# A Swin window block on one core: scores of four images at once, gelu as one image and then three, and the values of a chunk made in the first half of its own period

## What is computed

```
xw = windows of x                                  # 64 tokens of 32 channels each
q, k, v = split(ln1(xw) @ qkv_w.T + qkv_b)         # 4 heads of 8
attn = softmax(q * hd**-0.5 @ k.T + bias)          # 64x64 for each window and head
xw = xw + (attn @ v) @ proj_w.T + proj_b
h = gelu(ln2(xw) @ fc1_w.T + fc1_b)                # 128 hidden
xw = xw + h @ fc2_w.T + fc2_b
```

## Time and profile before

| | us |
|---|---|
| median of 3 runs | 189.28 |
| lowest, highest | 188.22, 192.5 |
| the profiled execution's own time | 188.29 |
| its span, first to last instruction | 186.6 |
| busy: PE, ACT, DVE, POOL | 169.2, 129.2, 120.2, 91.4 |
| TensorE's granted clock, mean | 0.998 of full speed |

### The profile page before, as it was taken

One profiled execution on the slowest core, in us unless ns is written; L12 is line 12 of the kernel. 1 busy time (PEld: TensorE's weight loads), 2 busy tenths in 40 slices (PEclk: granted clock), 3 DMA queues, 4 the chain that ended last, 5 costly groups with the idle time before them and its releaser, 6 DMA issues.

```text
span 186.6 us, 6349 instructions
## 1 busy us (share of the span) xinstructions
PE 169.2 (91%) x2688; PEld 92.4 (50%) x2688; DVE 120.2 (64%) x220; ACT 129.2 (69%) x180; POOL 91.4 (49%) x103
## 2 busy tenths in 40 slices
PE   7976999999999999999999999999999878738882
PEld 7642465566456546565565565455655533102210
DVE  3486965978687677869786977677697821403222
ACT  4546595569677866868696779677843385798881
POOL 7402674647492856567484937584766540020000
PEclk9999999999999999999999999999999999999999
DMA  2840000000000000000000000000000000001323
GB/s 71 231 174 4 0 2 4 4 4 2 4 4 0 4 4 2 4 5 0 4 4 4 0 4 5 0 4 0 4 5 4 0 4 0 29 27 56 116 112 112
DMA packets 3245, 4.71 MB, mean 25 GB/s; under 512 B 946, under 2 KB 1298, under 8 KB 3218
## 3 DMA queue, kind: packets, MB, share of 16 engines
q1 hardware_dynamic: 2840, 4.23, 6.7%
q0 software_dynamic: 256, 0.07, 0.4%
q10 hardware_dynamic: 122, 0.01, 0.0%
HBM read 2.21 MB, written 2.10 MB: 23 GB/s over the span
## 4 chain that ended last, share of the span: by engine, by line
PE 67%; DVE 10%; ACT 10%; issue 5%; DMA 3%; POOL 3%; ACTq 1%; DVEq 0%; POOLq 0%
PE ps L670 17%; PE ps L686 12%; PE ps L605 9%; PE ps L704 9%; PE ps L711 7%; DVE s_sb L477 7%; ACT hid L342 5%; PE ps L651 4%; PE ps L751 4%; PE ps L629 3%; DMA raw_b<-in_L_conv_rpb_dram 3%; POOL raw_b L193 2%; DVE mx L487 1%; ACT rstd L330 1%; ACT pt L255 1%
## 5 line engine op out<-in xcount | busy, mean ns | idle before, releaser
L211 POOL TENSOR_TENSOR s_sb<-s_sb,mx 128x512 f32<-128x512 f32 x64 | 66.6, 1045 | 61.1 <-DVE mx L487 61.1
L477 DVE TENSOR_TENSOR s_sb<-ps,bias_t 128x512 f32<-128x512 f32 x64 | 43.9, 686 | 26.0 <-PE ps L670 25.0
L487 DVE TENSOR_REDUCE mx<-s_sb 128x8 f32<-128x512 f32 x64 | 43.9, 686 | 2.2
L670 PE MATMUL ps<-k_m,q_sb 32*64 32x256 f32 x512 | 35.0, 387 | 2.9 <-DVE s_sb L477 2.1
L686 PEld LDWEIGHTS ps<-ident,s_sb 128*128 128x128 f32 x256 | 27.5, 140 | 17.7 <-issue 10.3
L255 ACT ACTIVATE pt<-ps 128x1024 f32<-128x1024 f32 x32 | 32.5, 1016 | 5.1 <-PE ps L686 4.2
L686 PE MATMUL ps<-ident,s_sb 128*128 128x128 f32 x256 | 34.9, 279 | 0.0
L670 PEld LDWEIGHTS ps<-k_m,q_sb 32*64 32x64 f32 x512 | 16.4, 131 | 15.2 <-DVE s_sb L477 5.6
L704 PEld LDWEIGHTS ps<-pt,v_blk 128*32 128x32 f32 x1024 | 15.0, 110 | 8.1 <-ACT pt L255 6.0
L704 PE MATMUL ps<-pt,v_blk 128*32 128x64 f32 x1024 | 17.6, 220 | 1.5 <-ACT pt L255 1.5
L342 ACT ACTIVATE hid<-ps,fb 128x1024 f32<-128x1024 f32 x16 | 17.0, 1110 | 2.0 <-PE ps L751 2.0
(11 more groups left out here) (92 smaller groups left out, 190.5 us busy)
## 6 DMA issues: line engine op xcount, KB each, us to landing
x_sb<-in_x_dram SPq DMA_DIRECT2D x8, 256.0 KB, 4.8
out_dram<-y_sb SPq DMA_DIRECT2D x7, 256.0 KB, 2.0
out_dram<-y_sb SPq DMA_DIRECT2D x2, 128.0 KB, 1.8
raw_b<-in_L_conv_rpb_dram POOLq DMA_DIRECT2D x8, 8.0 KB, 2.7
f_nat<-in_L_conv_fc_w_dram SPq DMA_DIRECT2D x2, 16.0 KB
w_nat<-in_L_conv_qkv_w_dram ACTq DMA_DIRECT2D x1, 12.0 KB
p_nat<-in_L_conv_proj_w_dram SPq DMA_DIRECT2D x1, 4.0 KB
vec_r<-in_L_conv_ln_g_dram ACTq DMA_DIRECT2D x1, 0.1 KB
```

What stands on the lines that cost most here:

```text
L211: pool.tensor_tensor(tile, tile, mx[:, n % 4, :].unsqueeze(2).to_broadcast([128, 2 * NH, NT]), ALU.subtract).then_inc(shifted, 1)
L477: dve.tensor_tensor(s_sb[:, n % NSB, :, :, :].rearrange("p a h m -> p a (h m)"), S_PS[u].rearrange("p (a k) -> p a k", a=2), bias_t[:, :, ...
L487: dve.reduce_max(mx[:, n % 4, :], s_sb[:, n % NSB, :, :, :].rearrange("p a h m -> p (a h) m"), AX.X)\
L670: ins = pe.matmul(S_PS[u][NT * ab:NT * (ab + 1), 256 * pr:256 * (pr + 1)], q_sb[C * g:C * (g + 1), c % 2, NT * w:NT * (w + 1)], k_m[C * g: ...
```

## The change

Eight units a chunk stay, but their scores are made in two calls of four images (`score(c, t)`, t the half of the windows), into four banks. That takes two banks more, so the others are shared anew: `S_PS` is banks 0 to 3, `T_PS` 4 and 5, and only `X_PS` (bank 6) and `Y_PS` (bank 7) are left. The first variance goes to score bank 0 between the scores' two calls, q to bank 0 behind the second, v to bank 1 between the calls, the first half of attention to bank 1 behind the second; the second normalization, the projection and the second half of attention are all in `Y_PS`. New waits guard the shared banks: among them `score(c, 0)` waits for `divided` of the chunk before, `score(c, 1)` for `v_copied` of its own chunk. v of chunk c is made in period c and not in period c-1. `inv_std2` is cut in two, with `exp_round` between its logarithm (`log_var2`) and its exponential. `gelu` reads one bank (the shared one) and then three. `up(0)` goes ahead of the last `attend`. Nothing else of the arithmetic changes.

The core of the diff:

```diff
-        S_PS = [ps[:, 0, :], ps[:, 1, :]]
-        T_PS = [ps[:, 2, :], ps[:, 3, :]]
-        FA, FB = ps[:, 4, :], ps[:, 5, :]
-        O_PS, D_PS = ps[:, 6, :], ps[:, 7, :]
-        OD_PS = [O_PS, D_PS]
...
+        S_PS = [ps[:, g, :] for g in range(G)]
+        T_PS = [ps[:, 4, :], ps[:, 5, :]]
+        X_PS, Y_PS = ps[:, 6, :], ps[:, 7, :]
+        OD_PS = [S_PS[1], Y_PS]
...
+        def unit_of(c, t, g):
+            return 8 * c + 4 * t + g
...
-            def inv_std2(p):
+            def log_var2(p):
                 act.wait_ge(var2_ready, p + 1)
                 if p >= 1:
                     act.wait_ge(h2_ready, p)
-                act.activation(rstd2[:, :], FB, ACT.Ln, bias=eps[:, :]).then_inc(log2, 1)
+                act.activation(rstd2[:, :], Y_PS, ACT.Ln, bias=eps[:, :]).then_inc(log2, 1)
+
+            def inv_std2(p):
                 act.wait_ge(log2, p + 1)
...
-                for pair in ((1, 0) if low(c) else (0, 1)):
-                    b = first_bank(c) + 2 * pair
-                    act.activation(hid[:, c % 2, 2 * pair:2 * pair + 2, :].rearrange("p g n -> p (g n)"),
-                                   ps[:, b:b + 2, :].rearrange("p g n -> p (g n)"),
+                shared = 3 - first_bank(c)
+                for images in (slice(shared, shared + 1), slice(0, 3) if low(c) else slice(1, 4)):
+                    banks = slice(first_bank(c) + images.start, first_bank(c) + images.stop)
+                    act.activation(hid[:, c % 2, images, :].rearrange("p g n -> p (g n)"),
+                                   ps[:, banks, :].rearrange("p g n -> p (g n)"),
                                    ACT.Gelu, bias=fb1[:, :]).then_inc(gelu_ready, 1)
...
-                if there(p):
-                    inv_den(p, 0)
                 if there(f):
                     square1(f)
                 if c == 0:
                     blank_values(1)
                 if there(p - 1):
+                    log_var2(p - 1)
+                if there(p):
+                    exp_round(p, 3)
+                if there(f):
+                    inv_std1(f)
+                if c >= 1 and there(c):
+                    copy_v(c)
+                if there(p - 1):
                     inv_std2(p - 1)
                 if there(p):
-                    exp_round(p, 3)
-                if there(f):
-                    inv_std1(f)
-                if there(p):
                     inv_den(p, 1)
-                if there(c):
-                    exp_round(c, 0)
-                if there(f):
-                    copy_k(f)
-                    if f == 0:
-                        copy_q(f)
-                    if f == 0:
-                        copy_v(f)
-                if there(c):
-                    exp_round(c, 1)
-                if f >= 1 and there(f):
-                    copy_v(f)
-                if f >= 1 and there(f):
-                    copy_q(f)
                 if p == NCH - 1:
                     act.preload_act_table_set("gelu_and_others")
                     gelu(0)
                     act.preload_act_table_set("natural_log_exp_and_others")
+                if there(c):
+                    exp_round(c, 0)
+                    exp_round(c, 1)
+                if there(f):
+                    copy_k(f)
+                    if f == 0:
+                        copy_q(f)
+                        copy_v(f)
+                if there(c):
+                    inv_den(c, 0)
+                if f >= 1 and there(f):
+                    copy_q(f)
                 if there(p):
                     square2(p)
                 if there(c):
...
                 if there(c):
-                    add_bias(c, 0, 0)
-                    find_max(c, 0, 0)
-                    add_bias(c, 0, 1)
-                    find_max(c, 0, 1)
-                if there(p):
-                    divide(p, 0)
-                if there(c):
-                    add_bias(c, 1, 0)
-                    find_max(c, 1, 0)
-                    add_bias(c, 1, 1)
-                    find_max(c, 1, 1)
+                    for g in range(G):
+                        add_bias(c, 0, g)
+                        find_max(c, 0, g)
                 if there(f):
                     norm1(f)
                 if there(p):
                     divide(p, 1)
                 if there(c):
-                    add_bias(c, 2, 0)
-                    find_max(c, 2, 0)
+                    for g in range(2):
+                        add_bias(c, 1, g)
+                        find_max(c, 1, g)
                 if there(p):
                     residual(p)
                 if there(c):
-                    add_bias(c, 2, 1)
-                    find_max(c, 2, 1)
-                    add_bias(c, 3, 0)
-                    find_max(c, 3, 0)
+                    for g in range(2, G):
+                        add_bias(c, 1, g)
+                        find_max(c, 1, g)
+                    divide(c, 0)
                 if there(p):
                     keep2(p)
-                if there(c):
-                    add_bias(c, 3, 1)
-                    find_max(c, 3, 1)
...
                 if f >= 1:
-                    pe.wait_ge(q_copied, f)
-                pe.matmul(FB, mean_m[:, :], sq1[:, :], start=True, stop=True).then_inc(var1_ready, 1)
+                    pe.wait_ge(biased, unit_of(f - 1, 0, 0) + 1)
+                pe.matmul(S_PS[0], mean_m[:, :], sq1[:, :], start=True, stop=True).then_inc(var1_ready, 1)
...
             def make_v(f):
+                if f >= 1:
+                    pe.wait_ge(biased, unit_of(f, 0, 1) + 1)
+                else:
+                    pe.wait_ge(log1, 1)
...
-            def score(c, r):
-                if r == 0:
+            def score(c, t):
+                if t == 0:
                     pe.wait_ge(q_copied, c + 1)
                     pe.wait_ge(k_masked, c + 1)
                     if c >= 1:
                         pe.wait_ge(k_scaled, c)
-                n = unit(c, r, 0)
-                if n >= 2:
+                        pe.wait_ge(divided, 2 * (c - 1) + 1)
+                    else:
+                        pe.wait_ge(v_copied, 1)
+                else:
+                    pe.wait_ge(v_copied, c + 1)
+                    if there(c + 1):
+                        pe.wait_ge(log1, c + 2)
+                n = unit_of(c, t, 0)
+                if n:
...
                 for pr in range(2):
                     for ab in range(2):
-                        w = 4 * (r // 2) + 2 * pr + ab
-                        for u in range(2):
-                            g = 2 * (r % 2) + u
-                            ins = pe.matmul(S_PS[u][NT * ab:NT * (ab + 1), 256 * pr:256 * (pr + 1)],
+                        w = 4 * t + 2 * pr + ab
+                        for g in range(G):
+                            ins = pe.matmul(S_PS[g][NT * ab:NT * (ab + 1), 256 * pr:256 * (pr + 1)],
...
-                if c == 0:
+                if t == 0:
+                    pe.wait_ge(biased, unit_of(c, 1, 1) + 1)
+                elif c == 0:
                     pe.wait_ge(late_ready, 1)
-                elif t == 0:
-                    pe.wait_ge(x1_ready, c)
                 else:
-                    pe.wait_ge(kept2, c)
+                    pe.wait_ge(log2, c)
...
-                if there(c):
-                    score(c, 1)
                 if there(f):
                     variance1(f)
-                if there(p):
-                    attend(p, 1)
+                if c >= 1 and there(c):
+                    make_v(c)
                 if p == NCH - 1:
                     up(0)
+                if there(p):
+                    attend(p, 1)
                 if there(c):
                     turn(c, 0)
-                    score(c, 2)
+                    score(c, 1)
+                    turn(c, 1)
                 if there(f):
                     wait_k(f)
                 if there(p):
@@ -814,11 +821,8 @@
                     make_k(f)
                 if there(p):
                     project(p)
-                if there(f):
-                    make_v(f)
-                if there(c):
-                    turn(c, 1)
-                    score(c, 3)
+                if there(c):
+                    attend(c, 0)
                 if there(f):
                     wait_q(f)
                 if there(p):
@@ -831,7 +835,6 @@
                     down(0, 4, slice(0, TC))
                 if there(c):
                     turn(c, 2)
-                    attend(c, 0)
```

More of the change, by code:

```diff
@@ L220, in _ @@
                 f = c + 1
[L221 to L226 removed]
+                if there(c):
+                    for g in range(G):
+                        subtract_max(c, 0, g)
+                if there(c - 2):
+                    norm2(c - 2)
+                if there(c):
+                    subtract_max(c, 1, 0)
                 if f >= 1 and there(f):
@@ L229, in _ @@
                 if there(c):
-                    subtract_max(c, 3, 0)
```

(4 more changed lines are left out.)

115 lines of the change are left out of this document (54 added, 61 removed).

## The result

| | before | changed |
|---|---|---|
| median, us | 189.70 (4 runs) | 177.43 (4 runs) |
| lowest, highest | 188.22, 192.5 | 176.41, 178.3 |
| the profiled execution's own time, span | 188.29, 186.6 | 178.3, 176.6 |
| ratio to before, 95% interval | | 0.938 (0.928 to 0.947) |

What follows compares the result with a forecast made beforehand. PE's groups in written order were taken as the bound, 17.32 us a period. Start +0.4, period 0 -2.4, period 1 -1.5, periods 2 to 6 -6.25, chunk 7 +0.1, MLP -1.3 turn 188.3 into 177.3; forecast 178, range 176 to 180.

Steps and rivals of the forecast that it cites:

- Score call: PE's call of four images, 16 matmuls on eight array parts: slot 1.05, between bounds 1.02 and 2.05.
- rival A: Score call: eight array parts do not run together; call 2.05, period 17.8, total 191.7 us; chance 0.12.
- The handover to DVE: From score start to first bias on DVE: 1.19 against 1.15 before, as four semaphore increments replace two.
- Wait at the turn of the period: Period start: `variance2` waits for `keep2` then `square2`, starting at 1.35 not 1.05; 0.3 of new wait.
- First half: From a chunk's first score to its second: PE's groups run on from 1.35, second score at 8.46.
- Second half: Second score to next first: DVE's four units, `residual`, `divide`, then 0.06 to PE; from 8.46 to 16.06.
- What ends the period: Period end: PE waits 0.2 for DVE's second half, ending in `divide`; period about 16.1 against 17.32.
- the signs that I had listed: Profile after: chain shows DVE's second half, rest PE; forecast falls if ACT holds whole stretches of a period.
- B: Period's turn: 0.2 more on each of `keep2`, `square2`, exponential or square; period 16.7, total 182 us; chance 0.19.
- C: Whole period: PE stays the bound throughout, its slots alone summing to 15.2; total 172.5 us; chance 0.05.
- Chunk 7's piece: From chunk 7's first score to the last `attend`: 19.75 against 19.64 before, +0.1 us.
- The MLP's -1.3: MLP: one bank first releases `up` earlier, chunks 2.12 and 2.33 apart instead of 2.45; -1.3 us.

Runs made afterwards that it cites:

- the best kernel: Changed kernel with both `divide` and `keep2` put ahead of the last unit's maximum on DVE; 173.53 us, ratio 0.918, again 173.77 us, 0.918.
- The forced 2.23: Changed kernel with two images' scores first, PE waiting until they end before the other two, so four parts work at once; 190.8 us, ratio 1.007.
- the second profile: Changed kernel run again unaltered, with another profiled execution; 176.57 us, ratio 0.935.
- both orders that were tried: Changed kernel's own matmul order in a score call, and changed kernel with two images whole before the other two; the latter 177.54 us, ratio 0.938.

## Why the prediction was right

**Score call.** 1.05 forecast, 1.05 found, where nothing waits behind it (106.44 - 105.39 in the best kernel). The forced 2.23 with its 190.8 us shows the mechanism, and sizes rival A: it had reckoned 17.8 and 191.7 for a call of 2.05, and the longer call gave 17.55, so A had its period too long. The handover to DVE is 102.08 - 100.90 = 1.18 for 1.19. But the reason that I gave for the 0.04 over the earlier trace rows, four increments in place of two, was misread: the fifth unit's `add_bias` waits for the first of the four only (`wait_ge(scored, n + 1)`), as it did when there were two, and the call's records last 1.12 for 1.09, which is the 0.03. So this row cannot test the rule on the semaphore tail that I cited (the Trainium skill, TensorE: Matmul & The Clock Gate, The cost: per-tile semaphore tail); no run here does.

**Wait at the turn of the period.** The step was right, its size off: 0.3 forecast, 0.1 found (1.15 from score to pair for 1.35), and in the forecast's order: `keep2`, `square2`, pair. I had the score 0.06 behind the end of `divide`, so that `keep2` ran beside it. But the score came 0.26 behind, 0.34 after `keep2` had started, and the chain from `keep2` on was already on its way: the late handover hid most of the wait. So the 0.2 less here and the 0.2 more in the second half are the same time, counted in another place.

**First half.** 8.46 forecast, 8.05 found: 0.2 from that wait, and 0.21 from two slots that were taken from neighbours of other shapes, the turn 0.92 for 1.03 and `variance1` 0.96 for 1.06.

**Second half.** 7.60 forecast, 7.79 found. Of it, 4 units with residual are 108.02 - 102.08 = 5.94, exactly 4 x 1.32 + 0.66, and `divide` 0.41; the 0.19 is the handover to PE, 0.26 for 0.06, which was a choice without a row. PE's own sum there, 15.9 for the period, was the nearer one, but for another reason: PE did wait, for DVE.

**What ends the period.** 16.06 forecast, 15.93 and 15.89 found. That PE ends up waiting for DVE by 0.2 holds, by 0.23, but the forecast put `divide` as the last link of the second half and `keep2` as a wait on top, where the ring through `keep2` sets the period and the score's wait for `divide` is not on it. Of the signs that I had listed, one did not come and one spoke against me: the chain does not show DVE's second half, and it does show ACT for a whole stretch of a period, 6 of 15.84 us, on which I had said the forecast would fall. It does not fall on it, since that row is level with PE's to 0.02 and the best kernel came down to 15.44 with the row as it was; but a forecast that rests on such a margin is near its edge.

**Rivals.** B put 0.2 more on each of the links `keep2`, `square2` and the exponential; none came. ACT's margins held, though its row in the first half has none left, as told above: in the second half the turn at 102.22 and the `attend` behind it wait 0.2 each for an exponential, as forecast, and the first half has no wait but that for `keep2`'s chain. C, PE the bound throughout at 15.2, is not reached by the change; moving `divide` and `keep2` comes within 0.24 of it, 15.44, though the forecast had said that only a DVE chain 0.9 shorter would do: DVE's work was not shortened, only put in another order.

**Ends.** Chunk 7's piece came 0.4 shorter than reckoned: 0.3 of it is the wait at the turn, which is not there at all (its pair stands 1.06 behind its score, for 1.35), and 0.1 lies behind its second score. The MLP's -1.3 is -1.57 at full clock and -0.3 in the profiled execution, where the low stretch took 1.3 back; at full clock two chunks take 4.37 us where 2.12 + 2.33 = 4.45 was forecast. The start's +0.4 was +0.3 in the second profile and +1.35 in the first, in which a group of set-up (L610 at 5.37) took 1.85 and not 1.08. That was not the clock, which is granted in full there; over the profiles of all variants the group takes from 1.07 to 1.91, and why is not shown. In that execution the start and the MLP were 0.95 and 1.0 longer than forecast, the periods and chunk 7 together 1.0 shorter; the sum missed by 1.0, 178.3 for 177.3. The second profile, low only in the first `down` (12.66 for 12.07), has a span of 174.6, where the sum stands for 175.6. The 0.7 between the sum and the forecast, for a median above the profiled execution, did not carry over from before: the median, 177.43, is 0.9 below it. So 178 was near in part by luck, because errors of both signs met; the mechanism, two score calls fewer a period with some of it kept by waits, is what the runs show.

## What to carry to other kernels

A group of small matmuls is priced by the parts of the array that it fills, not by its number: here sixteen on eight parts took 1.05 where eight on four had taken 1.02, and forced apart they cost the whole gain. When a link of a ring is shortened and the time stays, write the starts of all links of three variants side by side; the one whose distance to the next stays constant (here `keep2` to the pair, 1.49) is the one to move. Take a slot from a row with neighbours of the same shapes, and a handover from a row with the same waits in the same order. Look in the code which of several increments a wait asks for before pricing the others. And where two paths are level, the chain shows one of them: compare its links with the timeline before calling them the bound.

## What the hardware showed that I had not expected

- Matmuls on free parts of the array started beside those ahead of them in both orders that were tried: 1.15 against 1.12 busy.
- A turn ahead of another group that uses the whole array has a slot of 0.92, ahead of 64-row groups or a score 1.02.
- The place of a wait among several of one instruction cost 0.11 here: 0.15 from DVE's end to PE's start with the last to come written last of five, 0.26 with it written fourth.
- The granted clock dropped after PE had idled for 2.43 us in the first profile of the changed kernel; in the second, after 2.42 us at the same place, the groups ran at full speed (1.14 for `up`). In that second profile the clock fell earlier, near 147.9, ahead of the first `down`, where PE had idled for 1.48 and 0.85 us around one group. Why one place and not the other stays open.
